# A graph network's preparation redone: edges packed in one integer, one table from SBUF, four gathers, first rows counted by TensorE, layer norm by statistics per tile

## The reference, cut to what matters

```python
edge_index = jnp.stack([src, dst])
h = jnp.maximum(_layernorm(x, axis=-1), 0.0)
x = x + _L0_gnn_ref(h, edge_index, ...)     # two layers
h = jnp.maximum(_layernorm(x, axis=-1), 0.0)
x = x + _L1_gnn_ref(h, edge_index, ...)     # U-net of nine convolutions
return x

# one layer of the first network
xn = _l2norm(h)
agg = jax.ops.segment_sum(xn[src], dst, num_segments=n)
out = _l2norm(agg) * h_norm * scale
out = _l2norm(out @ Wl + bl + h @ Wr)

# one convolution of the second
h = x @ W
agg = jax.ops.segment_sum(h[src] * norm[:, None], dst, num_segments=n)
agg = agg + h * (1.0 / deg)[:, None] + b
```

## Time and profile before

| | before |
|---|---|
| time, median of 3 runs | 1281.97 us (1281.82 to 1282.44) |
| the profiled execution's own time | 1276.17 us |
| its span | 1274.3 us |
| mean granted TensorE clock | 0.891 |
| busy: PE, PEld, DVE, ACT, POOL | 954.8, 629.2, 595.6, 394.6, 85.9 us |
| start of the build (first L936) | 96.03 us |

### The profile page before, as it was taken

The page is one execution under the profiler, slowest core; times in us unless marked ns, Lnnn a source line. Parts: engine busy times, 40 slices in busy tenths (PEclk is TensorE's granted clock), DMA queues, the critical chain, the costliest instruction groups (busy, mean ns, idle before and its releaser), DMA issues.

```text
span 1274.3 us, 17689 instructions
## 1 busy us (share of the span) xinstructions
PE 954.8 (75%) x7283; PEld 629.2 (49%) x7283; DVE 595.6 (47%) x1588; ACT 394.6 (31%) x839; POOL 85.9 (7%) x105
## 2 busy tenths in 40 slices
PE   0035899998689999979979688385696575668796
PEld 0024666667355556955455374264454443434553
DVE  4769999983950011730140264255252453333312
ACT  0136889881340000550020140255102411220400
POOL 2300000000000000000000003312004200020000
PEclk9999999997879999869989889697897677779799
DMA  7611000008000000020000006264013300040101
GB/s 265 216 30 52 2 2 1 2 2 322 1 1 1 1 1 1 2 104 1 1 1 1 0 1 191 58 198 146 1 29 82 92 1 2 26 154 9 44 2 53
DMA packets 43046, 66.72 MB, mean 52 GB/s; under 512 B 4017, under 2 KB 33902, under 8 KB 42315
## 3 DMA queue, kind: packets, MB, share of 16 engines
q1 hardware_dynamic: 34196, 43.70, 10.1%
q0 software_dynamic: 4848, 18.65, 4.8%
q10 hardware_dynamic: 3910, 3.12, 0.9%
HBM read 39.78 MB, written 35.25 MB: 59 GB/s over the span
## 4 chain that ended last, share of the span: by engine, by line
PE 48%; DVE 33%; ACT 6%; issue 5%; another core or an unknown queue 4%; DMA 3%; POOL 0%; DVEq 0%; ACTq 0%; POOLq 0%; SPq 0%
PE psum L2526 22%; PE psum L2050 11%; DVE region L943 8%; DVE region L936 6%; PE psum L2301 2%; PE psum L2494 2%; PE psum L2413 2%; PE psum L2377 1%; DVE region L1390 1%; PE psum L2059 1%; DMA half_table<-region 1%; DVE region L891 1%; PE psum L2368 1%; DVE region L992 1%
## 5 line engine op out<-in xcount | busy, mean ns | idle before, releaser
L2526 PE MATMUL psum<-adj,region 128*128 128x448 fp8e4 x1050 | 201.4, 353 | 0.0
L2526 PEld LDWEIGHTS psum<-adj,region 128*128 128x128 f16 x1050 | 102.9, 98 | 93.3 <-issue 0.2
L2050 PE MATMUL psum<-adj,region 128*128 128x448 fp8e4 x700 | 134.0, 355 | 0.9 <-ACT region L1750 0.9
L1989 PE MATMUL psum<-region 128*128 128x200 bf16 (+2 forms) x1176 | 109.8, 228 | 31.5 <-DVE region L943 31.5
L1989 PEld LDWEIGHTS psum<-region 128*128 128x128 bf16 x1176 | 92.0, 98 | 69.2 <-DVE region L943 43.8
L1812 ACT ACTIVATE region<-psum 128x512 fp8e4<-128x512 f32 (+5 forms) x116 | 65.3, 603 | 124.4 <-PE psum L2436 40.3
L2050 PEld LDWEIGHTS psum<-adj,region 128*128 128x128 f16 x700 | 68.8, 98 | 66.1 <-issue 1.8
L943 DVE TENSOR_TENSOR region<-iota_key,region 128x1200 bf16<-128x1200 bf16 x147 | 101.3, 743 | 0.0
L1720 ACT ACTIVATE adj<-psum 128x400 fp8e4<-128x400 f32 x196 | 88.3, 508 | 28.5 <-PE psum L1993 28.2
L736 POOL DMA_INDIRECT region<-adj_table,node_of x33 | 32.0, 970 | 932.0 <-DVE node_of L1516 808.5
L1390 DVE CAST region<-psum 128x512 fp8e4<-128x512 f32 (+2 forms) x87 | 47.7, 598 | 100.5 <-PE psum L2368 60.1
(11 more groups left out here) (330 smaller groups left out, 1277.3 us busy)
## 6 DMA issues: line engine op xcount, KB each, us to landing
adj_table<-adj SPq DMA_DIRECT2D x1, 10000.0 KB, 26.9
src_table<-in_src SPq DMA_DIRECT2D x1, 4656.0 KB
dst_table<-in_dst SPq DMA_DIRECT2D x1, 4656.0 KB
region<-dk_dram SPq DMA_DIRECT2D x2, 1568.0 KB, 8.4
adj_table<-region SPq DMA_DIRECT2D x1, 2704.0 KB, 8.6
half_table<-region SPq DMA_DIRECT2D x2, 832.0 KB, 5.7
node_table<-region SPq DMA_DIRECT2D x1, 1650.0 KB, 8.0
xs_dram<-nodebuf SPq DMA_DIRECT2D x1, 1600.0 KB, 5.9
```

The lines of the kernel that those rows point to most:

```text
L1989: pe.matmul(psum[:, q % BUILD_BANKS, i * KEYS + k0:i * KEYS + k1], hot_lo[:, r, c, j, :, i], hot_key[:, r, c, j, k0:k1, i], start=(n == 0) ...
L2050: last = pe.matmul(psum[:, b, 0:BLOCK], weight(t, k), adj[:, t * PAD + b * BLOCK:t * PAD + (b + 1) * BLOCK], start=(t == 0 and k == 0), st ...
L2526: last = pe.matmul(psum[:, b, 0:width], here[:, t, k, :], rows, start=(t == 0 and k == 0), stop=(t == n_src - 1 and k == 1))
```

## The change

The change rewrites the preparation only. The diff, cut to its core:

```diff
+EDGE_COLS = EC + SLOTS - GRAIN        # 800 + 384 - 32 = 1152
+LASTS = EC // GRAIN                   # 25
+PACK = 4096
@@ sync
-            sp.dma_start(dst_in, a["dst"].rearrange("(p c) -> p c", p=EP)).then_inc(edges_in, DMA)
-            sp.wait_ge(last_picked, 1)
-            sp.dma_start(last_row.rearrange("(p c) -> p c", p=EP), last_in).then_inc(last_out, DMA)
-            sp.wait_ge(last_out, DMA)
-            sp.dma_start(last_all, last_row.rearrange("(o c) -> o c", o=1).broadcast_to((P, EDGES // GRAIN))).then_inc(last_back, DMA)
-            for table, edges in ((src_table, a["src"]), (dst_table, a["dst"])):
-                for r0, r1 in ((0, ROWS // 16 * 16), (ROWS // 16 * 16, ROWS)):
-                    rows = bass.AP(edges.tensor, r0 * GRAIN, [[GRAIN, r1 - r0], [1, SLOTS]])
-                    sp.dma_start(table[r0:r1, :], rows).then_inc(table_in, DMA)
+            for to, edges in ((dst_in, a["dst"]), (src_in, a["src"])):
+                sp.dma_start(to[0:EP - 1, :], bass.AP(edges.tensor, 0, [[EC, EP - 1], [1, EDGE_COLS]])).then_inc(edges_in, DMA)
+                sp.dma_start(to[EP - 1:EP, 0:EC], row_of(edges[(EP - 1) * EC:EDGES])).then_inc(edges_in, DMA)
+            sp.wait_ge(edges_packed, 1)
+            for p0, p1, rows in ((0, EP - 1, LASTS), (EP - 1, EP, ROWS - (EP - 1) * LASTS)):
+                at = packed[p0:p1, :]
+                sp.dma_start(edge_table[p0 * LASTS:p0 * LASTS + (p1 - p0) * rows, :].rearrange("(p r) s -> p r s", r=rows),
+                             bass.AP(at.tensor, at.offset, [at.ap[0], [GRAIN, rows], [1, SLOTS]])).then_inc(table_in, DMA)
@@ gpsimd (also: iota_window and ones_h are made first)
-            pool.wait_ge(table_in, 4 * DMA)
+            pool.wait_ge(table_in, 2 * DMA)
             for g in range(GROUPS):
-                for rows, table in ((edge_src, src_table), (edge_dst, dst_table)):
-                    pool.indirect_dma_start(out=rows[:, g, :], ...).then_inc(gathered[g], DMA)
+                pool.indirect_dma_start(out=edge_rows[:, g, :], out_offset=None, in_=edge_table, ...).then_inc(gathered[g], DMA)
@@ vector
-            dve.wait_ge(edges_in, DMA)
-            nc.vector.tensor_copy(last_in, ...).then_inc(last_picked, 1)
             nc.vector.memset(nodebuf[:, PAD - P:PAD], 0.0).then_inc(pads_zeroed, 1)
-            dve.wait_ge(last_back, DMA)
-            for g in range(GROUPS):
-                step(nc.vector.tensor_scalar(compared, last_all, win_base[:, g:g + 1], 0.0, ALU.is_lt, ALU.add,
-                                             accum_out=row_f[:, g:g + 1]))
+            dve.wait_ge(edges_in, 4 * DMA)
+            nc.vector.scalar_tensor_tensor(packed[:, 0:EC], dst_in[:, 0:EC], float(PACK), src_in[:, 0:EC], ALU.mult, ALU.add)
+            nc.vector.scalar_tensor_tensor(packed[0:EP - 1, EC:EDGE_COLS], ..., ALU.mult, ALU.add).then_inc(edges_packed, 1)
+            step(nc.vector.tensor_scalar(last_window, ..., 3, None, ALU.logical_shift_right))
+            step(nc.vector.tensor_copy(last_f, last_window))
             dve.wait_ge(x_in, 2 * DMA)
-            layernorm(nodebuf[:], nodebuf[:], region3[:, 0:PAD], 1).then_inc(h0_ready, 1)
+            for t in range(TILES):
+                last = nc.vector.bn_stats(stats[:, t, :], tiles(nodebuf[:])[:, t, :])
+            ...                             # mean and variance of 25 columns, rsqrt
+            nc.vector.scalar_tensor_tensor(shift, shift, -0.5, inv, ALU.mult, ALU.mult).then_inc(centered, 1)
+            dve.wait_ge(more_consts, 2)
+            for c in range(LASTS):
+                nc.vector.tensor_scalar(later[:, c, :], iota_window[0:EP, :], last_f[:, c:c + 1], None, ALU.is_gt).then_inc(windows_compared, 1)
+            dve.wait_ge(windows_counted, 1)
+            nc.vector.tensor_scalar(row_i[:]..., psum[:, 4:4 + GROUPS, 32:33], float(ROWS - 1), None, ALU.min).then_inc(rows_known, 1)
             dve.wait_ge(h0_squared, 1)
             ...                             # reduce, inverse_norms, scaled0 as before
+            edge_keys(0)                    # one operation more than before: dest = edge_rows >> 12
+            dve.wait_ge(hi0_ready, 1)
+            nc.vector.tensor_tensor(parts0[:, :, 1, :], ..., ALU.subtract).then_inc(parts0_ready, 1)
+            for g in range(1, GROUPS):
+                edge_keys(g)
@@ scalar
             act.wait_ge(centered, 1)
-            nc.scalar.activation(region3[:, 0:PAD], nodebuf[:], ACT.Square).then_inc(squared, 1)
+            for t in range(TILES):
+                last = nc.scalar.activation(x, x, ACT.Relu, bias=tiny[:, 0, t:t + 1], scale=tiny[:, 1, t:t + 1])
+            last.then_inc(h0_ready, 1)
             act.wait_ge(h0_ready, 1)
             nc.scalar.activation(region3[:, 0:PAD], nodebuf[:], ACT.Square).then_inc(h0_squared, 1)
+            ...                             # the seven copies to h0t, from banks 4 to 6
             act.wait_ge(scaled0, 1)
@@ tensor
+            pe.wait_ge(more_consts, 2)
+            for c in range(LASTS):
+                pe.wait_ge(windows_compared, c + 1)
+                for g in range(GROUPS):
+                    last = pe.matmul(psum[:, 4 + g, 32:33], later[:, c, g * P:(g + 1) * P], ones_h[0:EP, 0:1], start=(c == 0), stop=(c == LASTS - 1))
+            last.then_inc(windows_counted, 1)
+            pe.wait_ge(rows_known, 1)
+            pe.wait_ge(h0_ready, 1)
+            ...                             # the 25 transposes of nodebuf, moved here from behind the keys
```

More of the change, by code:

```diff
@@ L723, in _ @@
             pool.wait_ge(rows_known, 1)
-            pool.wait_ge(table_in, 4 * DMA)
+            pool.wait_ge(table_in, 2 * DMA)
             for g in range(GROUPS):
-                for rows, table in ((edge_src, src_table), (edge_dst, dst_table)):
-                    pool.indirect_dma_start(out=rows[:, g, :], out_offset=None, in_=table,
-                                            in_offset=bass.IndirectOffsetOnAxis(ap=row_i[:, g:g + 1], axis=0)
-                                            ).then_inc(gathered[g], DMA)
+                pool.indirect_dma_start(out=edge_rows[:, g, :], out_offset=None, in_=edge_table,
+                                        in_offset=bass.IndirectOffsetOnAxis(ap=row_i[:, g:g + 1], axis=0)).then_inc(gathered[g], DMA)
             pool.wait_ge(flag_ready, 1)
@@ L909, in _ @@
-            for g in range(GROUPS):
-                dve.wait_ge(gathered[g], 2 * DMA)
-                low, high = work[0].bitcast(I32), work[1].bitcast(I32)
-                late, outside = work[2], work[3]
+            dve.wait_ge(edges_in, 4 * DMA)
+            nc.vector.scalar_tensor_tensor(packed[:, 0:EC], dst_in[:, 0:EC], float(PACK), src_in[:, 0:EC], ALU.mult, ALU.add)
+            nc.vector.scalar_tensor_tensor(packed[0:EP - 1, EC:EDGE_COLS], dst_in[0:EP - 1, EC:EDGE_COLS], float(PACK), src_in[0:EP - 1, EC:EDGE_COLS],
+                                           ALU.mult, ALU.add).then_inc(edges_packed, 1)
@@ new lines, in _, with edge_keys @@
+            dve.wait_ge(h0_squared, 1)
+            step(nc.vector.tensor_reduce(ss, tiles(region3[:, 0:PAD]), AX.X, ALU.add))
+            inverse_norms(unit, norm0, ss)
+            step(nc.vector.tensor_scalar(unit, unit, UNIT_SCALE, None, ALU.mult))
+            nc.vector.tensor_tensor(tiles(region3[:, PAD:2 * PAD]), tiles(nodebuf[:]), per_node(unit), ALU.mult).then_inc(scaled0, 1)
+            def edge_keys(g):
+                dve.wait_ge(gathered[g], DMA)
+                low, high, dest = (work[k].bitcast(I32) for k in range(3))
+                late, outside = work[3], work[4]
@@ L913, in _ @@
                 loc = key_rows[:, g, :]
[L914 to L916 removed]
+                nc.vector.tensor_scalar(low, edge_rows[:, g, :], P - 1, None, ALU.bitwise_and)
+                nc.vector.tensor_scalar(high, edge_rows[:, g, :], 7, PACK // P - 1, ALU.logical_shift_right, ALU.bitwise_and)
@@ L1695, in _ @@
                                          ACT.Copy).then_inc(by_edge_ready, 1)
-            for g, (t0, n) in enumerate(GROUPS4):
-                act.wait_ge(h0_turned, g + 1)
-                nc.scalar.activation(h0t[:, t0 * P:(t0 + n) * P], psum[:, g % 4, 0:n * P], ACT.Copy).then_inc(h0t_ready, 1)
             act.sem_inc(bank_free, BUILD_BANKS)
@@ L1938, in _ @@
         def _(pe):
-            pe.wait_ge(consts_ready, 11)
+            pe.wait_ge(more_consts, 2)
[4 more added lines that the diff above has]
+            last.then_inc(windows_counted, 1)
+            pe.wait_ge(consts_ready, 11)
+            pe.wait_ge(rows_known, 1)
+            pe.wait_ge(h0_ready, 1)
+            for g, (t0, n) in enumerate(GROUPS4):
+                if g >= 3:
+                    pe.wait_ge(h0t_ready, g - 2)
+                for t in range(t0, t0 + n):
+                    last = pe.transpose(psum[:, 4 + g % 3, (t - t0) * P:(t - t0 + 1) * P], nodebuf[:, t * P:(t + 1) * P], ident[:])
+                last.then_inc(h0_turned, 1)
             for g in range(GROUPS):
```

(7 more changed lines are left out.)

80 lines of the change are left out of this document (43 added, 37 removed).

## The result

The changed kernel takes 1313.01 us, the median of 4 runs (1311.58 to 1316.03), against 1281.89 for the kernel before on the same chip. The ratio is 1.026, with a 95% interval of 1.0236 to 1.0284. I had forecast 1252, and given 2 in 100 to slower. The profiled execution took 1314.31 us, its span is 1312.4 and its mean granted clock 0.855.

The account below looks back on a forecast made before the run. No one engine bounds the whole; the preparation ahead of VectorE's build sets its start. New steps bring that from 96.0 to 66.0 us, 30 less: 1281.97 - 30 = 1252 us, range 1246 to 1261.

Parts of the forecast that it names:

- The table and its gathers: SP's store of the 4.78 MB table, allowed 17 us, landing at 28; first gather there at 37, wanted at 43.8.
- Inputs: Start of the kernel: edges land at about 9.5 us, x at 11.7, packing done at 11.3.
- The table becomes the bound: Rival: store at 114 GB/s takes 42 us, lands at 53; build at 81, 1267 us; chance 0.07.
- the clock: Rival: TensorE's granted clock gives the time back; a mean 0.06 lower makes 1292 us; chance 0.02.
- Statistics: Layer norm on VectorE: 25 BN_STATS of 128 elements at 0.20 us each, 5.0 us in all.
- ScalarE's 25: Normalisation by tile, 25 activations on ScalarE taking 9.8 us, ending at 30.2.
- comparisons: Counting on VectorE beside ScalarE: 25 of 512 elements at 0.35 us, 8.8 us in all, hidden.
- TensorE's 100 products: Counting: four one-column products after each of 25 comparisons, 9.5 us in all, up to 21.7.
- a key group: Keys ahead of the build: each of four groups takes 4.04 us, 3.67 before plus one operation and its wait.
- the low part: Step on VectorE between the first group's keys and the other three groups: 3.5 us, from 47.8 to 51.3.
- The reduction waited for ScalarE: Sign: VectorE's reduction after the squares should wait for ScalarE, not TensorE; otherwise the forecast is wrong.
- I count an earlier start as a gain in full: Assumption: the list behind the build's start is unchanged, so its 30 us earlier start shortens the time by 30.

Follow-up runs that it names:

- e2: Changed kernel with only the loads of both edge lists cut into 112, 12 and 1 rows, store unchanged; 1266.62 us, ratio 1.0177.
- e3: Changed kernel with both the edge loads and the table's store cut into 112, 12 and 1; 1215.95 us, ratio 0.9765.
- e5: e3 with the last 53 rows of x loaded as 48 and 5; 1257.6 us, ratio 0.9817.
- e8: The kernel before with its two tables copied in 3100 + 14 rows instead of 3104 + 10; ratio 0.9993.
- e11: e9 with ScalarE waiting for x ahead of its five loads of weights; 1250.44 us, ratio 0.9757.
- e6: e3 with the old layer norm in place of the statistics and ScalarE's 25 activations; 1255.07 us, ratio 0.9787.
- e9: e3 with x loaded ahead of the edges on SP's queue, statistics before packing, squares in two parts; 1250.1 us, ratio 0.9772.
- e12: e10 with the five loads of weights issued behind ScalarE's layer norm; 1252.05 us, ratio 0.9779.
- e1: Changed kernel with only the table's store cut into 112, 12 and 1 partitions, loads unchanged; 1227.1 us, ratio 0.9856.
- e7: e3 with the transposes of the nodes and their seven copies moved back behind the keys; 1259.95 us, ratio 0.982.
- e4: Changed kernel with loads cut as in e3 and the store in 119, 5 and 1 partitions; 1236.46 us, ratio 0.9926.
- e10: e3 run once more, unchanged, on another chip; 1257.22 us, ratio 0.98.

## Why the prediction was wrong

**The step that failed** is "The table and its gathers": "By size alone mine takes 13; I allow 17 for shorter pieces, so it lands at 28". The store was priced by its bytes against the 10 MB row. It ran on 4 of 16 engines, took 76.8 us from 26.07 and landed at 102.89. The same error stands in "Inputs": the edges "at about 9.5" came at 23.7, since their loads too have 124 partitions; in e2, with the loads mended, they came at 12.85. Undone together they bring the build to 69.0, 3.0 from the forecast's 66.0. One alone is not enough: with the store mended the late edges still cost 11.3 us (80.3), with the loads mended the store costs 47.2 (116.2).

**The rival had the right mechanism and a wrong price.** "The table becomes the bound" put the point of decision at a landing after 37.7, with 28.3 us from landing to build. Measured: landing at 102.89, build 26.3 later, POOL's first issue being 1.12 us rather than 2.95. It took the other store from SBUF as the worst case, 42 us and a landing at 53; mine took 77. I bounded an unknown transfer by the two rates in the trace, and neither was a bound: both stores have 128 partitions, and the 10 MB one ran at a share of 0.95, nearly all 16 engines. The case ended on the slow side, where I had put only the clock.

**The other steps held.** Statistics 4.93 for 25 (5.0 forecast); from there to `centered` 3.7 (3.7); ScalarE's 25 in 9.72 (9.8); comparisons 6.64 (8.8); TensorE's 100 products 6.47 (9.5); row numbers at 41.08, ahead of the squares, which end at 46.8; a key group 4.04 (4.04); the low part 3.48 (3.5). The comparisons and the products were priced a third and nearly a half too high, which ScalarE's cover hid. The path in e3 from `centered` at 23.9 to the build at 69.0 is 45.1 us where the forecast has 45.6. The reduction waited for ScalarE, 5.62 us, as it was to. The Trainium skill, "VectorE: DVE Perf Modes", section "The perf-mode tier table", gives the forecast's estimate of 0.29 us for a comparison; the trace has 0.266 (6.64/25), 8% less. By its section "The TRN2 errata" one of ScalarE's activations of 128 is estimated at 0.293 us; the trace has 0.389 (9.72/25), and the measurement decides. *Inputs* stayed too cheap even with all engines: in e3 x landed at 15.2, not 11.7, at 238 and 229 GB/s from 4 to 8 and from 8 to 12 us, where I had taken 306 to 390, though the engines were as good as full (shares 1.01 and 1.04). These 3.5 us, less the 0.5 by which the path behind was shorter, are the 3.0 that are left.

**The clock did not do it.** The mean fell from 0.891 to 0.855. By the rival's own sum (0.045 for 31 us) that would cost 25 us. But the fall lies in the front. Windows of before and of after, from the start of the build to the end:

```profile
96.03:1274.30 1178.27, 944.32 (x7233) 620.62 (x7233) 536.81 (x1492) 377.33 (x819) 69.76 (x73) 0.88 0.13 43
```

```profile
129.23:1312.40 1183.17, 956.69 (x7233) 626.39 (x7233) 536.35 (x1492) 378.33 (x819) 69.85 (x73) 0.87 0.13 41
```

Ahead of the build the mean went from 1.00 to 0.70: the row from 60 to 90 us shows 0.50, half of full speed, in a stretch in which TensorE had no work. (The rival's time for a mean lower by 0.06 should be 1293 by its own numbers, not 1292; nothing hangs on it.) The part behind the start of the build (span less build) is 1183.2 us after and 1178.3 before; in e5 to e8 on one chip the same difference varies from 1179.5 to 1188.3, so 4.9 us can't be told from no change. In the build's first 20 us the clock was still at 0.61 and 0.73, and VectorE, which bounds it, was busy throughout.

**The gain was real.** In the changed kernel and all twelve experiments the time moved with the start of the build, to within 4.2 us: +33.2 and +31.1 after, -27.0 and -30.1 in e3, -30.0 and -31.1 in e11. "I count an earlier start as a gain in full" was right to within these 4 us. A difference of 5 us, as between e5 and e6, is not shown to pass on in full.

## What to carry to other kernels

Before a transfer is priced by its bytes, look at the size of its slowest dimension on both sides, and work out the largest divisor up to 16; the DMA share of a window, times 16, shows afterwards how many engines ran. What is measured here is SP's queue with 4, 7, 10 and 16 engines. Price it as pieces for each engine by the time of a piece, and take that for a rough price: a piece took 77 to 99 ns on the four engines of one store. Where the number is small, split off the rest so that the bulk has a multiple of 16. And when a transfer is moved ahead, look at what other queues still have to issue beside it: a held issue stops the engine that makes it.

## What was not expected of the hardware

**A queue's issue can be held, it seems by another queue's transfer.** The five loads of weights took 2.5 to 3.4 us to issue on ScalarE in the six runs where they ran wholly outside the time of the table's store: 2.5 in the changed kernel (22.01 to 24.47), in e2, in e9 (4.39 to 6.85, with x in flight) and in e12, 2.8 in e11, 3.4 in e1. Beside the store of 4.8 MB they took 4.7 in e7, 6.1 in e3, 6.4 in e5, 8.9 in e4 and 11.6 in e10. That the store holds them is argued from this order. What sets the size between 4.7 and 11.6 is open, and no run moves the store alone. The Trainium skill, "DMA: Bandwidth & Descriptors", section "Issuing engines are not separate DMA queues", calls the time of an issue usually small; here it put ScalarE 7.6 us behind its release in e10. Between e3, where it did no harm, and e10 the edges' landing differs by 2 us.

**Chips differ where gathers do.** The kernel before took 1246.0 us on the chip of e1 to e4 and 1279.62 to 1281.89 wherever else it ran. The part behind the build was 1144.5 to 1149.5 us there, and 1177.7 to 1188.3 elsewhere, with the same instructions. The view of the tile `adj_table` shows a difference that goes with it, in e3 and in e10, us to landing of its 33 gathers and two stores:

```profile
DMA to landing us min/median/max: 3.1/4.7/28.1
```

```profile
DMA to landing us min/median/max: 3.8/8.1/28.1
```

On the first chip the median is 4.7 to 4.9 in all four kernels, elsewhere 7.9 to 8.3 in all ten. The largest of them, the 10 MB store, took 28.1 in both. The chain of e10 has a piece that e3's lacks, and one of 50.8 to 51.0 us is found in all ten runs on the other chips and in none of the four:

```profile
747.81 50.88 another core or an unknown queue
```

It lies right where these gathers are: the first ones start at 761.79. The issues of SP's stores show where the 38.4 us between e3 and e10 behind the build come in. From the build to the store of `node_table` the two differ by 1.0 us (670.5 and 671.5). From there to the first store of `half_table`, while the first 26 gathers run, e10 takes 20.0 longer (43.2 and 63.2). Over the next two such stretches, with 27 gathers, it takes 7.8 longer each, and in all that follows, with the last 20, only 1.8. So most of it arises where the first 53 gathers are. That they are its cause is argued from this and not shown, and why one chip has them quicker stays open. It is the reason to compare only kernels run on the same chip.
